# New tables of places for the last two batches and the expert tiles of a two-layer transformer kernel

## What is computed

```python
x = L0_attn_x                                   # (16, 512, 128)
xn = _layernorm(x, axis=-1)
x = x + _L0_attn_ref(xn, ...) + _L0_ffn_ref(xn, ...)
xn = _layernorm(x, axis=-1)
x = x + _L1_attn_ref(xn, ...) + _L1_ffn_ref(xn, ...)

# the experts of layer 1
for e in range(num_experts):
    h = x @ w1[e]
    a, g = jnp.split(h, 2, axis=1)
    y = jax.nn.silu(a) * g @ w2[e]
    out = jnp.where((max_ind == e)[:, None], y, out)
out = out * max_prob
```

## Time and profile before

| | |
|---|---|
| time, median of 3 runs | 1230.09 us (1229.64 to 1230.7) |
| the profiled execution | 1230.84 us, span 1229.3 us, mean granted clock 0.977 |
| TensorE busy | 1148.4 us, 93% of the span |
| VectorE, ScalarE busy | 903.0 us, 901.8 us, 73% each |
| GpSimd busy | 637.3 us, 52% |
| busy in tenths, TensorE, 40 slices | 6768999999999999999999999999997889899998 |
| granted clock in tenths, 40 slices | 9778999999999999999999999999998899999999 |
| chain that ended last | PE 73%, ACT 12%, DVE 7%, issue 5%, POOL 2% |

### The profile page before, as it was taken

How to read it: one execution, slowest core, us unless ns; L and a number is a source line. 1 busy time by engine, 2 the same in 40 slices (tenths; PEclk the granted TensorE clock), 3 DMA queues, 4 the chain that set the end, 5 groups by cost and what they waited for, 6 DMA issues and landing times.

```text
span 1229.3 us, 28397 instructions
## 1 busy us (share of the span) xinstructions
PE 1148.4 (93%) x9744; PEld 681.6 (55%) x9744; DVE 903.0 (73%) x2439; ACT 901.8 (73%) x1224; POOL 637.3 (52%) x857
## 2 busy tenths in 40 slices
PE   6768999999999999999999999999997889899998
PEld 3344454545454545455454545454543466799997
DVE  4548888888888888888888888888879573345554
ACT  3133887878787888788888878787875868567775
POOL 2342646474646565555646464746463202048886
PEclk9778999999999999999999999999998899999999
DMA  4660607142442526060607061524464400024543
GB/s 149 173 129 14 129 17 164 43 104 70 78 101 46 117 38 126 22 135 12 137 10 137 16 131 43 105 68 78 102 182 81 126 23 11 19 44 63 62 58 31
DMA packets 94378, 98.10 MB, mean 80 GB/s; under 512 B 12432, under 2 KB 74384, under 8 KB 93840
## 3 DMA queue, kind: packets, MB, share of 16 engines
q1 hardware_dynamic: 81536, 86.72, 31.9%
q0 software_dynamic: 12272, 8.92, 5.6%
q10 hardware_dynamic: 432, 0.66, 0.1%
HBM read 68.98 MB, written 26.23 MB: 77 GB/s over the span
## 4 chain that ended last, share of the span: by engine, by line
PE 73%; ACT 12%; DVE 7%; issue 5%; POOL 2%; DMA 0%; ACTq 0%; DVEq 0%; POOLq 0%
PE PS L801 11%; PE PS L686 11%; PE PS L841 10%; PE PS L638 6%; PE PS L768 6%; PE PS L786 5%; PE PS L852 5%; ACT flow L955 4%; ACT L955 3%; PE PS L630 3%; PE PS L652 2%; DVE nm L1224 2%; PE PS L753 2%; PE PS L619 2%; ACT early L879 2%
## 5 line engine op out<-in xcount | busy, mean ns | idle before, releaser
L1396 POOL TENSOR_SCALAR_AFFINE_SELECT flow<-flow 128x256 f32<-128x256 f32 (+1 forms) x448 | 192.1, 442 | 342.9 <-ACT flow L955 340.0
L955 ACT ACTIVATE flow<-PS 128x1024 f32<-128x1024 f32 x320 | 319.6, 1027 | 43.2 <-PE PS L786 35.7
L1224 DVE TENSOR_REDUCE nm<-PS 128x2 f32<-128x1024 f32 x128 | 154.8, 1221 | 64.3 <-PE PS L753 57.2
L946 ACT COPY qp<-PS 4x1024 f16<-4x1024 f16 x128 | 128.2, 1002 | 64.7 <-PE PS L776 63.6
L801 PE MATMUL PS<-flow 128*32 128x512 f32 (+3 forms) x2048 | 168.4, 448 | 2.5 <-POOL flow L1396 1.0
L686 PE MATMUL PS<-early,down 128*128 128x512 f32 x288 | 148.8, 629 | 9.5 <-POOL early L1381 9.5
L1381 POOL TENSOR_TENSOR early<-early 128x512 f32<-128x512 f32 x120 | 152.5, 1293 | 7.5 <-DMA early<-gate_rows 7.2
L638 PE MATMUL PS<-xnT,up 128*128 128x512 f32 x288 | 146.8, 613 | 0.0
L1420 POOL DMA_INDIRECT out_y<-X,rowu x71 | 110.5, 1556 | 60.1 <-DMA out_y<-X 33.6
L841 PE MATMUL PS<-xsT,w1s 128*128 128x128 f32 x1136 | 139.2, 276 | 1.2 <-DVE act L1323 1.1
L1320 DVE SCALAR_TENSOR_TENSOR tanh<-tanh,PS 128x512 f32<-128x512 f32 x71 | 48.8, 688 | 120.7 <-ACT tanh L989 102.8
(11 more groups left out here) (164 smaller groups left out, 1985.4 us busy)
## 6 DMA issues: line engine op xcount, KB each, us to landing
early<-gate_rows SPq DMA_DIRECT2D x128, 256.0 KB, 4.6
qp<-relay_q SPq DMA_DIRECT2D x64, 128.0 KB
kp<-relay_k SPq DMA_DIRECT2D x64, 128.0 KB
xsb<-xs SPq DMA_DIRECT2D x71, 65.0 KB, 2.0
relay_k<-qkh SPq DMA_DIRECT2D x32, 128.0 KB
out_y<-X SPq DMA_DIRECT2D x16, 256.0 KB, 2.6
early<-in_w SPq DMA_DIRECT2D x1, 4096.0 KB, 13.4
relay_q<-qkh SPq DMA_DIRECT2D x16, 128.0 KB, 2.3
```

The costliest lines, as they stand in the source:

```text
L946: ins = act.copy(m.qp[b % 2][at:at + MR, 2 * g:2 * g + 2, :], rows)
L955: act.activation(m.pt[:, n % RING, :], m.PS[:, i:i + 2, :].rearrange("p k c -> p (k c)"), ACT.Exp, scale=1.0 / SCALE).then_inc(s["exp"], 1)
L1224: dve.tensor_reduce(nm[:, 3, 2 * n:2 * n + 2], ps, AX_X, ALU.max, negate=True).then_inc(s["max"], 1)
L1396: ins = pool.affine_select(part, part, [[0, part.shape[1]], [1, P]], ALU.is_ge, nothing, base=0, channel_multiplier=-1)
```

## The change

Three tables are replaced, and no function. `LAST` gets new places, up to about the 44th tile (before, up to the 31st, and regular behind it). `OWN` gave tables to batches 0, 1 and 2; those of 1 and 2 held the common places, that of 0 differed from them in two. They go, and batches 15 and 14 get `AT_E1` and `AT_E2`. Every step is still there, once. Since the file is 38 lines shorter ahead of the functions, a line of the changed kernel is 38 lower than the same line before.

```diff
 LAST = placed(
-    w1=[-30.389],
-    w2=[-4.773],
+    w1=[-36.754],
+    w2=[-11.713],
...
-    load=[-8.748, -8.482, -7.999, -7.83, -7.464, -7.35, -6.024, -5.111, -4.921, -4.495, -4.338, -2.457, -2.41, -2.398,
+    load=[-11.478, -11.469, -9.204, -8.943, -7.491, -7.157, -7.102, -6.805, -6.781, -4.262, -3.786, -2.629, -1.213,
...
-    rows=[-2.364, -1.829, 3.217, 3.656, 4.683, 4.891, 5.115, 7.778, 9.47, 11.828, 12.734, 12.879, 12.901, 16.78,
+    rows=[-7.053, -3.453, 2.714, 3.251, 5.476, 5.904, 6.774, 6.875, 7.778, 10.677, 10.962, 11.904, 13.917, 16.882,
...
-AT_B0 = placed(
...
-    parts=[-24.018, -22.9],
-    relay=[-22.7],
...
+AT_E1 = placed(
...
+    parts=[-23.801, -19.647],
+    relay=[-17.494],
...
-OWN = {0: AT_B0, 1: AT_B1, 2: AT_B2}
+OWN = {B - 1: AT_E1, B - 2: AT_E2}
```

More of the change, by code:

```diff
@@ L272 @@
-AT_B1 = placed(
-    stats0=[-58.434],
-    norm0=[-49.057],
-    xnT0=[-47.786],
-    kvr=[-46.922, -45.731, -45.728, -44.77],
-    up=[-42.665, -40.737, -38.785, -38.501, -38.442, -36.876, -36.66, -35.489, -34.449],
-    q=[-41.751],
-    kv=[-41.331],
-    route0=[-42.986],
-    gate=[-40.422],
-    attn0=[-40.173],
-    gT=[-39.945],
-    at0T=[-37.944],
-    down=[-34.855, -34.751, -33.817, -32.425, -31.899, -29.133, -29.051, -28.731, -28.704],
-    gated=[-37.556, -37.32, -36.942, -36.647, -36.101, -34.957, -32.339, -31.588],
-    x1=[-27.643],
-    stats1=[-27.25],
-    norm1=[-25.94],
-    xnT1=[-25.658],
-    rope=[-24.551, -22.979],
-    parts=[-24.018, -19.749],
-    relay=[-17.917],
-    v=[-19.073],
-    logits=[-22.589],
-    route1=[-20.324],
-    expert=[-19.589],
-    ranks=[-17.997],
-    sort=[-17.769, -17.734, -13.635, -9.004],
-    score=[-0.564, 0.586, 1.58, 2.991, 5.933, 7.014, 8.967, 11.029, 12.082, 12.383, 13.463, 13.778, 14.269, 14.456,
-           14.546, 15.259, 15.756, 16.515, 16.659, 19.311],
-    max=[-9.041, -7.953, -6.62, -4.139, -2.021, -1.624, -1.614, 0.197, 0.722, 1.959, 3.077, 4.319, 4.552, 4.716,
-         5.126, 5.74, 6.973, 8.306, 9.706, 10.424],
-    mparts=[-1.774, 2.116, 7.241, 10.658],
-    mrows=[-1.374, 5.213, 10.556, 11.149],
-    value=[2.676, 9.758, 12.387, 14.034, 14.669, 16.226, 18.235, 20.306],
-    sums=[13.94, 20.393],
-    heads=[15.117, 21.524],
-    mT=[22.491],
-    out=[24.369],
-    store=[26.41])
@@ new lines @@
+    turned=[-3.859, -2.189, -0.602, 1.34, 3.286, 6.107, 6.238, 8.118, 9.762, 10.953, 10.989, 13.558, 14.559, 16.238,
[5 rows of a table added]
+    hidden=[-0.715, 1.29, 2.737, 3.351, 5.582, 6.879, 8.112, 9.198, 10.722, 11.563, 13.763, 14.647, 15.819, 17.348,
[4 rows of a table added]
+    outputs=[0.292, 3.355, 4.787, 6.03, 7.156, 8.288, 9.363, 10.93, 12.137, 14.227, 15.096, 17.429, 17.541, 19.621,
[5 rows of a table added]
+    scatter=[20.293, 21.231, 22.026, 22.461, 25.245, 25.431, 26.616, 26.989, 27.649, 28.11, 28.113, 28.277, 30.612,
[4 rows of a table added]
+NBETWEEN = 22
+AT_E1 = placed(
+    stats0=[-58.471],
+    norm0=[-48.613],
+    xnT0=[-47.796],
+    kvr=[-46.754, -45.731, -45.722, -44.824],
+    up=[-42.298, -40.996, -38.698, -38.501, -38.475, -36.112, -36.089, -35.549, -34.448],
+    q=[-41.751],
+    kv=[-41.091],
+    route0=[-42.828],
+    gate=[-40.27],
+    attn0=[-40.135],
+    gT=[-39.966],
+    at0T=[-37.078],
+    down=[-34.829, -34.314, -33.864, -32.521, -31.717, -29.053, -28.857, -28.479, -28.425],
+    gated=[-38.068, -37.725, -36.791, -36.182, -34.565, -33.031, -31.544, -30.204],
+    x1=[-27.902],
+    stats1=[-27.111],
+    norm1=[-26.573],
+    xnT1=[-25.726],
+    rope=[-24.36, -23.095],
+    parts=[-23.801, -19.647],
+    relay=[-17.494],
+    v=[-18.714],
+    logits=[-22.427],
+    route1=[-20.06],
+    expert=[-19.826],
+    ranks=[-17.735],
+    sort=[-18.164, -16.092, -15.756, -12.734],
+    score=[-0.139, 0.586, 2.202, 2.897, 6.971, 7.634, 8.253, 10.74, 12.038, 12.618, 12.778, 13.781, 14.345, 14.395,
+           14.762, 14.989, 15.288, 16.878, 17.462, 19.905],
+    max=[-8.992, -7.177, -6.458, -5.272, -2.917, -1.69, -0.854, -0.076, 1.253, 1.903, 2.993, 3.311, 4.662, 4.739,
+         4.903, 5.457, 7.558, 8.125, 10.076, 10.581],
+    mparts=[-1.873, 3.023, 7.933, 11.284],
+    mrows=[-1.032, 5.221, 10.584, 11.548],
+    value=[3.429, 9.5, 12.108, 13.957, 15.15, 17.299, 18.597, 20.311],
+    sums=[14.419, 20.901],
+    heads=[15.34, 21.867],
+    mT=[22.701],
+    out=[24.148],
+    store=[25.896])
@@ new lines @@
+AT_E2 = placed(
+    stats0=[-58.272],
+    norm0=[-48.912],
+    xnT0=[-47.853],
+    kvr=[-46.784, -45.729, -45.712, -44.871],
+    up=[-42.948, -40.903, -38.925, -38.597, -38.429, -36.5, -35.719, -35.489, -34.387],
+    q=[-41.658],
+    kv=[-41.211],
+    route0=[-42.982],
+    gate=[-41.053],
+    attn0=[-40.208],
+    gT=[-39.904],
+    at0T=[-37.409],
+    down=[-34.859, -34.506, -33.577, -32.38, -32.187, -29.365, -29.048, -28.652, -28.09],
+    gated=[-39.375, -37.448, -37.165, -35.945, -34.729, -34.087, -33.459, -31.111],
+    x1=[-27.707],
+    stats1=[-26.787],
+    norm1=[-26.272],
+    xnT1=[-25.667],
+    rope=[-24.25, -22.554],
+    parts=[-24.014, -19.674],
+    relay=[-18.162],
+    v=[-18.801],
+    logits=[-22.142],
+    route1=[-20.455],
+    expert=[-19.476],
+    ranks=[-17.239],
+    sort=[-18.594, -16.121, -13.467, -8.084],
+    score=[0.111, 0.679, 1.702, 2.266, 5.932, 7.298, 9.101, 10.417, 12.019, 12.491, 13.31, 13.363, 14.3, 14.586,
+           14.788, 14.93, 14.981, 15.996, 16.725, 19.26],
+    max=[-8.917, -8.111, -6.578, -4.217, -2.582, -1.388, -0.91, 0.298, 1.273, 1.722, 2.014, 3.148, 4.523, 4.709,
+         5.629, 5.713, 6.866, 7.969, 8.751, 10.652],
+    mparts=[-2.388, 2.339, 7.087, 10.682],
+    mrows=[-1.273, 4.203, 11.088, 12.612],
+    value=[2.748, 9.985, 12.872, 13.853, 14.767, 16.064, 17.999, 20.036],
+    sums=[13.696, 21.292],
+    heads=[15.22, 22.55],
+    mT=[22.874],
+    out=[24.496],
+    store=[23.166])
```

88 lines of the change are left out of this document (4 added, 84 removed), and 59 rows, old and new, of tables (hidden, load, outputs, rows).

## The result

| | before | after |
|---|---|---|
| median | 1229.93 us (1229.64 to 1230.7, 4 runs) | 1239.32 us (1238.9 to 1239.94, 4 runs) |
| profiled span | 1229.3 us | 1237.4 us |
| VectorE busy, ScalarE busy | 903.0 us, 901.8 us | 909.4 us, 900.9 us |
| mean granted clock | 0.977 | 0.977 |

The changed kernel is slower: ratio 1.0070, 95% interval 1.0058 to 1.0081, some 9 us. The forecast was 1229.4 us with a range up to 1236.0, so the time lies outside it, beyond the slower rival's 1234.

The account below looks back on a forecast made before the run. TensorE was taken as the limit, with idle time to win or lose only at the start, the batch 14 to 15 passage and the mixed stretch. -2.0 + 3.5 - 2.2 = -0.7 us gave 1229.4 us, range 1223 to 1236.

Parts of the forecast that it names:

- the slower rival: Load 0 lands after 968 and the waiting cast costs 6 us, start and mixed stretch give less: about 1234, chance 0.31.
- What bounds the kernel: TensorE is full from 140 to 850 us; only idle time at start, batch 14 to 15 passage and mixed stretch matters.
- Start: Batch 0: without its own table, batch 1's gates come earlier, the relay later; first `max` resumes earlier: -2.0 us.
- Batches 14 and 15: Up to 956 us: `expert` moved ahead delays the last relay's key half by about 2.0 us; TensorE loses 0 us.
- The lists' front: Early cast waits for load 0 and holds VectorE; TensorE stands 3.1 us at batch 15's fourth `max`, plus clock: +3.5 us.
- When is load 0 in: Landing of load 0 at the lists' front: 966.0 to 967.0 us after delays by relay and store, 966.5 taken.
- When does TensorE get there: TensorE done with the two scores ahead of batch 15's fourth `max` at about 964.9 us.
- The clock: Lower TensorE clock behind the wait at batch 15's fourth `max`: 0.4 us, from the 0.80 in 920 to 970 us.
- Such a place is not in this trace: Said the earlier trace shows no load queued behind `w2`; ring order would put load 0 at about 967.0, +0.5 us.
- The mixed stretch: 970 to 1095 us: some dearer waits between neighbours sharing a bank get work between them: -2.2 us.
- The end: Final scatters on GpSimd: 5.2 us are free, so output 20 falling behind one more `hidden` (1.8 us) is hidden: 0 us.
- The faster rival: TensorE late at the fourth `max` or SyncE keeping its times hides the wait: -5 us, about 1225, chance 0.33.

Follow-up runs that it names:

- experiment 4: Changed kernel with only batch 0's own table put back (key half and relay early): 1240.66 us, ratio 1.0081.
- experiment 6: Kernel before with `OWN` empty, so only batch 0's own table goes: 1231.17 us, ratio 1.0002.
- experiment 13: The kernel of experiment 10 with batch 0's own table put back: 1230.1 us, ratio 0.9991.
- experiment 10: Changed kernel with tile 0's cast late, `w2` behind two loads, and batch 15's `expert` behind `parts` again: 1230.17 us, ratio 0.9992.
- experiment 1: Changed kernel with only tile 0's `rows` cast moved back, behind the fourth `max` and the heads: 1231.39 us, ratio 1.0005.
- experiment 2: Changed kernel with only `w2` moved back behind nine loads, the cast still early: 1235.54 us, ratio 1.0036.
- experiment 14: The kernel of experiment 10 with the pads ahead of the store of batch 13: 1229.74 us, ratio 0.9993.
- experiment 11: Changed kernel with only `w2` moved behind the first two loads, the cast still early: 1233.62 us, ratio 1.0035.
- experiment 5: Kernel before with only tile 0's cast moved early, ahead of batch 15's third `max`; `w2` still behind nine loads: 1230.58 us, ratio 1.0000.
- experiment 8: Kernel before with the new list `LAST` and the tables of before: 1248.63 us, ratio 1.0144.
- experiment 12: Changed kernel with tile 0's cast between batch 15's third and fourth `max`, `w2` still ahead of the loads: 1237.8 us, ratio 1.0061.
- experiment 9: Changed kernel with tile 0's cast late and `w2` behind the first two loads: 1231.16 us, ratio 1.0002.
- experiment 3: Changed kernel with both tile 0's cast late and `w2` behind nine loads: 1238.25 us, ratio 1.0059.

## Why the prediction was wrong

**What bounds the kernel:** right. All that changed lies in the three places named; 140 to 850 us is the same to 0.01 us of TensorE's time.

**Start (-2.0):** the steps came in the order written, and the gates were back in 2.05 us, but two sizes were off and cancelled. The gates went out at 67.28 and not 70.1: 1.1 us of that is this execution's head start, and the attention matmuls ahead of them took 2.21 us where they had taken 4.18 (at 64.22, before at 68.08). The relay then took 25.0 us and not 22.1. So "in at 92.2" (92.26 by the trace) is luck. TensorE was there at 85.96 and not 89.8, and stood 6.30 us. The missing step is the price of that: its next work ran slowly (3.41 instead of 1.98 us), and from 50.7 us on nothing was gained at 97.5. Experiments 4, 6 and 13 find nothing in the time.

**Batches 14 and 15 (0):** the 2.0 us on the relay were right (experiment 10), also that TensorE hardly sees them: it is idle 12.2 us between 850 and 960, before 11.8.

**The lists' front (+3.5):** this is the step that failed: +3.5 us forecast, over 9 us measured. The mechanism was right, three of its terms were too small. *When is load 0 in:* taken 966.5, measured 969.80. I took the issue near 964 plus the landing time of the loads of before, though I had written that `w2` is issued first; the queue was treated as if a small load could pass it. 1.0 of the 3.3 us is the later issue, 2.3 the landing. *When does TensorE get there:* taken 964.9, measured 963.16 (962.77 + 0.39); I read it off the old order and at the old clock. One score that stood behind the third `max` is now ahead of it, and the 24 `flow` matmuls between them take 1.50 us at 960.23 where they took 2.79:

```profile
961.44 2.79 PE L801 MATMUL PS<-flow 128*32 128x384 f32 x24
```

The granted clock from 957 to 965 us was 0.57 before and 1.00 in the changed kernel. These two are 3.3 + 1.7 = 5.0 us, which is what 8.13 exceeds 3.1 by. *The clock:* taken 0.4, some 3.3 by experiment 1. I had read the 0.80 of the earlier trace rows as the worst; that row is a mean over idleness of at most 1.8 us, and over stretches at either clock. The size of the stall does not excuse this term: with 2.90 us of idleness, less than the 3.1 forecast, experiment 2 paid the clock in full.

"Such a place is not in this trace", as the prediction says of a load behind `w2`, was an oversight. In the kernel before, loads 9 to 11 are issued behind it (from 973.26 on). The line of the earlier trace rows does not show them, since it covers only two of the sixteen loads. By the semaphore records in the trace they were in at 980.27 to 980.65, right behind `w2` (980.08) and up to 7.0 us after their issue.

On the Trainium skill's rule ("DMA: Bandwidth & Descriptors", section on queues, rings and completion order), that descriptors of a queue are consumed in ring order: the trace agrees, and the prediction gave it +0.5 us beside the sum. The same section says that a DMA's increment of its semaphore lands only after every earlier write from that DMA engine; that too puts the load's end behind `w2`'s, and the traces do not tell the two apart. By either, the load is in when `w2` is, and the remaining error of that sentence was `w2`'s own time: 8.0 us taken, 10.6 measured, which gives 969.6.

**The mixed stretch (-2.2):** too much. TensorE's idle time between 970 and 1090 us fell as forecast, by 1.7 us in the changed kernel (15.05 to 13.32) and by some 3 in experiments 10, 13 and 14, but the time by 1 us at most. That idle time and time are one for one there was assumed; where the rest goes was not followed.

**The end (0):** right (at its pitch the last scatter could have started at 1221.0, not 1220.9). The scatters keep their pitch of 1.86 us up to the 66th and wait for outputs only behind it (before: behind the 65th); the last one follows TensorE's last `outputs` (1231.73) by 2.4 us in both kernels.

**The rivals.** The slower one had this mechanism and the point from which it decides ("load 0 lands after 968"; it was 969.8), and priced it 6 us where it is over 9. The faster rival failed in its condition: TensorE came early, not late, and SyncE did not keep its times.

| term | predicted | measured |
|---|---|---|
| start | -2.0 | +0.4 in the profile (46.8 to 46.4 us), 0 in the time |
| load 0 in | 966.5 | 969.80 |
| wait at the fourth `max` | 3.1 | 8.13 (1.82 of it would have been waited at `turned`) |
| low clock behind it | 0.4 | about 3.3 |
| mixed stretch | -2.2 | about -1, `w2` and the cast mended |
| sum | -0.7 | +9.4 in the medians, +8.6 in the tail |

The cause closes in the tail: experiment 1, with the late cast, is 0.7 us shorter than before (348.60 to 349.27), and from there to the changed kernel it is 9.3 (5.5 of idle time, 3.7 of clock).

## What to carry to other kernels

Before a small load is given a time, look at what stands ahead of it in its own queue: it comes in when that is in, whatever its own size. An operation that waits for a DMA belongs on an in-order engine behind all that others wait for; 0.15 us of work placed two steps too early cost 9 us here, 2.5 us with the load early (experiment 11), and nothing where TensorE also came late to the step behind it (experiment 5). And price a stall on TensorE with the clock behind it: here some 3 us after 8.13 us of idleness and as much after 2.90, nothing that shows after 0.93 and 1.82.

## What the runs showed of the hardware

**A load behind 2 MB in the same queue.** In the five kernels with `w2` right ahead of the loads, load 0 was issued 5.8 to 7.2 us after `w2` and was in at the end of `w2` each time, to 0.3 us:

| kernel | `w2` issued + landing | load 0 issued | used by its first waiter |
|---|---|---|---|
| changed kernel | 958.96 + 10.6 = 969.56 | 965.07 | 969.80 |
| experiment 1 | 958.84 + 10.7 = 969.54 | 965.18 | 969.79 |
| experiment 4 | 957.57 + 10.9 = 968.47 | 963.74 | 968.69 |
| experiment 8 | 959.48 + 11.0 = 970.48 | 966.64 | 970.70 |
| experiment 12 | 960.37 + 11.2 = 971.57 | 966.21 | 971.84 |

With `w2` behind it the load was in after 1.8 us (experiments 5 and 11) or 2.3 us (experiment 2). Where `w2` is third (experiments 9, 10, 11, 13 and 14), the slowest load behind it takes 7.1 to 8.0 us to land, so other small loads behind the 2 MB come late too.

**The same 2 MB took two durations.** 10.6 to 11.2 us right behind the pads, in all five; 7.8 to 9.0 us behind loads, in the eleven others. Whether the writes of the lists, which had just gone out, or the wider spread of its issue (1.22 us against 0.34 to 0.47 us) are the reason was not tried, and stays open.

**The clock behind a stall.** After 8.13 us of idleness TensorE was granted 0.51 of its clock over the next ten microseconds; the work was back at its usual durations at 979.97 (0.39 us for four matmuls of 384 columns). After 2.90 us in experiment 2 it was granted 0.50 over 967 to 977, and was back at 977.10. After 3.48 us in experiment 3 the first `outputs` took 2.07 us and not 1.16. After 6.30 us in batch 0 the next four large matmuls took 1.7 times their time. After 1.82 us in experiment 1 the work behind ran at its usual durations (0.39 us for the same four at 970.08), and after 0.93 us in experiment 11 as well (1.00 over 967 to 982).
